# Graph layers beside an attention of 128 blocks: layer steps spread over the slots, projection in the pieces' bank, two node buffers, two lent rows in every block with raw tiles

## What is computed

```python
# layers 0, 2, 3: degree-normalized aggregation, then a 128x128 projection
adj_norm = d[:, :, None] * adj * d[:, None, :]        # d = row sum (of adj + eye, |adj + eye|, or adj) ** -0.5
f = einsum('bnm,bmf->bnf', adj_norm, x) @ W + b
# layer 1: additive attention, masked where adj <= 0
q, k = x @ WQ, x @ WK
score[i, j] = p . relu(q[j] + k[i])                   # 2048 x 2048 x 128 terms for each graph
f = softmax(score + mask) @ x
```

## Time and profile before

| | |
|---|---|
| median of 3 runs | 13884.19 us (13881.76 to 13884.51) |
| the profiled execution's span | 13883.0 us |
| TensorE busy | 12956.7 us, 93% |
| VectorE busy | 13327.1 us, 96% |
| ScalarE busy | 12942.7 us, 93% |
| GpSimd busy | 1095.3 us, 8% |
| TensorE's granted clock, mean | 0.989 |

### The profile page before, as it was taken

One profiled execution on the slowest core, in us unless ns is written; L12 is line 12 of the kernel. 1 busy time (PEld: TensorE's weight loads), 2 busy tenths in 40 slices (PEclk: granted clock), 3 DMA queues, 4 the chain that ended last, 5 costly groups with the idle time before them and its releaser, 6 DMA issues.

```text
span 13883.0 us, 318102 instructions
## 1 busy us (share of the span) xinstructions
PE 12956.7 (93%) x143877; PEld 5442.7 (39%) x143877; DVE 13327.1 (96%) x14041; ACT 12942.7 (93%) x8528; POOL 1095.3 (8%) x706
## 2 busy tenths in 40 slices
PE   7889989999899999999999998999989999899988
PEld 3333434443344333444334443344434444333333
DVE  7999999999999999999999999999999999999995
ACT  6999999999999999999999999999999999999994
POOL 0000000010000100010000100001100010000000
PEclk9999999999999999999999999999999999999999
DMA  4111112221122112221122211222112221011103
GB/s 144 52 46 49 50 58 84 89 63 44 61 90 90 59 37 74 86 87 56 44 72 86 84 59 37 77 87 84 59 36 82 84 80 58 32 49 52 43 12 111
DMA packets 680284, 918.70 MB, mean 66 GB/s; under 512 B 60432, under 2 KB 421904, under 8 KB 659472
## 3 DMA queue, kind: packets, MB, share of 16 engines
q1 hardware_dynamic: 678928, 898.35, 20.7%
HBM read 705.23 MB, written 184.55 MB: 64 GB/s over the span
## 4 chain that ended last, share of the span: by engine, by line
DVE 56%; PE 34%; ACT 7%; issue 2%; DMA 1%; POOL 0%; SPq 0%; DVEq 0%; POOLq 0%; ACTq 0%
DVE big L1110 50%; PE score L1269 24%; ACT big L861 6%; PE acc L1183 5%; PE acc L1242 2%; PE turn L1154 2%; DVE att L1048 2%; DVE big L1090 1%; DVE gx L997 1%; DMA piece<-adj_turned 0%; DVE gx L976 0%; PE turn L1213 0%; DVE stats L984 0%; ACT q_pair L769 0%; DVE att L1037 0%
## 5 line engine op out<-in xcount | busy, mean ns | idle before, releaser
L1110 DVE TENSOR_SCALAR big<-q_pair,k_pair_cols 128x2048 f32<-128x2048 f32 x10029 | 12094.2, 1278 | 289.8 <-PE score L1269 272.4
L861 ACT ACTIVATE big<-q_f,k_cols 128x2048 f32<-128x2048 f32 x6060 | 11633.5, 1998 | 256.9 <-PE score L1269 247.5
L1269 PE MATMUL score<-big,unit_window 128*32 128x512 f16 x82592 | 5439.0, 394 | 750.3 <-DVE big L1110 716.7
L1269 PE MATMUL score<-big,sign_window 128*32 128x512 f32 x48480 | 5591.5, 595 | 69.2 <-ACT big L861 67.5
L1269 PEld LDWEIGHTS score<-big,unit_window 128*32 128x32 bf16 x82592 | 2308.1, 96 | 3952.0 <-DVE big L1110 1128.8
L1269 PEld LDWEIGHTS score<-big,sign_window 128*32 128x32 f32 x48480 | 1572.3, 110 | 3299.2 <-issue 2948.4
L1183 PE MATMUL acc<-piece,q_f 128*128 128x512 f32 x2944 | 1411.5, 602 | 18.1 <-DVE q_f L959 10.7
L668 POOL TENSOR_SCALAR att_var<-att_mom 128x1 f32<-128x1 f32 x128 | 73.4, 573 | 9809.0 <-DVE att_mom L1066 9809.0
L1183 PEld LDWEIGHTS acc<-piece,q_f 128*128 128x128 f32 x2944 | 503.1, 190 | 529.8 <-issue 470.2
L1242 PE MATMUL acc<-x,att_turned 128*128 128x128 f32 x4096 | 559.4, 280 | 0.0
L1242 PEld LDWEIGHTS acc<-x,att_turned 128*128 128x128 f32 x4096 | 504.1, 194 | 56.8 <-issue 56.8
(11 more groups left out here) (95 smaller groups left out, 2876.3 us busy)
## 6 DMA issues: line engine op xcount, KB each, us to landing
piece<-adj_turned SPq DMA_DIRECT2D x1472, 256.0 KB, 2.7
att<-in_adj_dram SPq DMA_DIRECT2D x128, 1024.0 KB, 5.2
q_pair<-in_adj_dram SPq DMA_DIRECT2D x240, 512.0 KB, 4.5
adj_turned<-q_pair SPq DMA_DIRECT2D x224, 512.0 KB, 4.8
adj_turned<-big SPq DMA_DIRECT2D x16, 1024.0 KB, 13.5
q_f<-in_adj_dram SPq DMA_DIRECT2D x16, 512.0 KB, 5.4
gx<-in_x_dram SPq DMA_DIRECT2D x32, 256.0 KB, 4.0
q_kept<-q_pair SPq DMA_DIRECT2D x32, 256.0 KB, 3.7
```

Source lines behind the costliest of these rows:

```text
L861: ins = nc.scalar.activation(ring["A"][:, RANK[g] % RING * 4 + u, :], q_of(c + 1), ACT.Relu, bias=k_cols[:, t % 2, QUAD * u + g:QUAD * u + ...
L1110: ins = nc.vector.tensor_scalar(ring["D"][:, RANK[g] % RING * 4 + u, :], pairs_of(c + 1), k_pair_cols[:, t % 2, QUAD * u + g:QUAD * u + g ...
L1269: ins = nc.tensor.matmul(score[QUAD * u:QUAD * (u + 1), cc, :], (unit_window if pair else sign_window)[:, QUAD - 1 - g:2 * QUAD - 1 - g], ...
```

## The change

The steps get places of their own. `STEP_END` gives for each step the place of its projection (70, 106, ... 454, each a slot); its 16 pieces are spread evenly over the slots from four places after the end before it (the first from 38) up to its own end, two or three to a slot. So twelve steps take 416 places instead of 384, and each slot in between has pieces, while the end slot itself has the projection. Copy and projection are at the end, the sum three or four places later, root, normalization and store at 5, 12, 13 after the end, and the second part of layer 0 (queries, keys) is moved to slots likewise. GpSimd's row beside the sum is in the group ahead of it instead of group 30. ScalarE's sum of a raw unit that would fall less than five places after an end is put to five after it. The projection goes to acc[1] in the batches with attention, so that a step's first piece waits for the sum of the step before, and `weigh` and `project` lose their waits on each other. `gx` and `x1` become two buffers that swap by batch; `keep_x1` goes; `load_x2` is one load for each step, three at place 28 and the last at 34. Every block with raw tiles lends two rows, 126 in all.

```diff
@@ -62,14 +62,55 @@
...
-    BLOCK = {"layer2": 2, "layer3": 6, "layer0": 10}
-    PIECES_AT = {-4: [0, 1, 2], 0: [3, 4, 5], 1: [6], 4: [7], 10: [8, 9], 14: [10], 18: [11], 23: [12, 13, 14, 15]}
-    SELF_AT, TURNED_AT, PROJECT_AT, SUM_AT, ROOT_AT, NORM_OUT_AT, STORE_AT = 18, 28, 28, 31, 33, 40, 41
-    SCALE_AT = {"layer2": [-25, -20, -15, -10], "layer3": [-5, -3, -1, 11], "layer0": [-5, -3, -1, 16]}
-    BIAS_AT, FIRST_LOAD_AT = 20, -8
...
-    X1_AT, X2_AT, X0_AT = 28, 34, 45
+    LAYERS = ("layer2", "layer3", "layer0")
+    STEP_END = {"layer2": [70, 106, 142, 174], "layer3": [210, 247, 279, 316], "layer0": [352, 384, 422, 454]}
+    FIRST_PIECE_AT = 38
+    ALL_SLOTS = [t * GROUPS + at for t in range(T) for at in SLOTS]
+    ENDS = [STEP_END[name][s] for name in LAYERS for s in range(STEPS)]
+    assert all(end in ALL_SLOTS for end in ENDS)
+
+    def slots_of(k):
+        first = FIRST_PIECE_AT if k == 0 else ENDS[k - 1] + 4
+        return [at for at in ALL_SLOTS if first <= at < ENDS[k]]
+
+    PIECE_PLACE = {(name, s): [slots_of(n * STEPS + s)[i * len(slots_of(n * STEPS + s)) // T] for i in range(T)]
+                   for n, name in enumerate(LAYERS) for s in range(STEPS)}
+
+    PROJECT_TIME = 5
+
+    def slot_from(place):
+        return min(at for at in ALL_SLOTS if at >= place)
+
+    def sum_offset(end):
+        return 4 if end % GROUPS == 0 else 3
+
+    SUM_PLACE = {(name, s): STEP_END[name][s] + sum_offset(STEP_END[name][s]) for name in LAYERS for s in range(STEPS)}
+    ROOT_AFTER, NORM_OUT_AFTER, STORE_AFTER, X0_AFTER, BIAS_BEFORE, LOAD_BEFORE = 5, 12, 13, 17, 8, 4
+    SCALE_PLACE = {"layer2": [31, 33, 35, 37],
+                   "layer3": [STEP_END["layer2"][-1] + at for at in (-1, 1, 3, 15)],
+                   "layer0": [STEP_END["layer3"][-1] + at for at in (-1, 1, 3, 20)]}
+    LOAD_PLACE = {"layer2": FIRST_PIECE_AT - 8, "layer3": STEP_END["layer2"][-1] - LOAD_BEFORE,
+                  "layer0": STEP_END["layer3"][-1] - LOAD_BEFORE}
+
+    def qk_places(s):
+        at = {"turn": slot_from(STEP_END["layer0"][s] + 17)}
+        at["copy"] = at["turn"] + 3
+        at["q"] = slot_from(at["turn"] + 4)
...
+        at["k"] = slot_from(at["q"] + 4)
...
+        return at
+
+    QK = [qk_places(s) for s in range(STEPS)]
+    X2_AT, X2_LAST_AT = 28, 34
...
 
...
@@ -292,7 +337,7 @@
         def lent_rows(c, t):
             if not units_where(c, lambda u: slot_place(2 * u) // GROUPS == t):
                 return []
-            return LENT_ROWS[:1 if steps_at(c, t * GROUPS + SELF_AT, SELF_AT) else 2]
+            return LENT_ROWS
 
         def lent_before(c, t, g):
             return sum(len(lent_rows(a, k)) for a in range(FIRST, c + 1) for k in range(T) if a < c or k < t) + \
@@ -350,7 +395,8 @@
 
         def sum_place(u):
             k = 2 * u
-            return k // len(SLOTS) * GROUPS + SUM_UNIT[SLOTS[k % len(SLOTS)]]
+            at = k // len(SLOTS) * GROUPS + SUM_UNIT[SLOTS[k % len(SLOTS)]]
+            return max([end + PROJECT_TIME for end in ENDS if end < at < end + PROJECT_TIME], default=at)
 
         def units_where(c, holds):
             if one_of(c, OPENING, LAST, CLOSING):
@@ -471,7 +523,7 @@
                 n = piece_of(c, name, s, i)
                 if n >= STEPS * T + PIECES:
                     sp.wait_ge(piece_used, piece_of(c, name, s, i, 1 - PIECES + AHEAD))
-                b = {"layer2": c, "layer3": c, "layer0": c + 2}[name]
+                b = batch_of(c, name)
                 sp.dma_start(piece[:, i % PIECES, :], adj_turned[b * (STEPS * T) + (s * T + i)]) \
                     .then_inc(piece_loaded[i % PIECES], 16)
 
@@ -494,28 +546,15 @@
             def load_x0(c, s):
                 if not one_of(c, OPENING, FIRST):
                     sp.wait_ge(out_stored, (c * STEPS + s + 1) * 16 + AHEAD)
-                if not one_of(c, OPENING):
-                    sp.wait_ge(x1_ready, (c + 2) * 16)
-                sp.dma_start(gx[:, s * PER:(s + 1) * PER, :], nodes[c + 2, :, s * PER:(s + 1) * PER, :]) \
+                sp.dma_start(nodes_of(c)[:, s * PER:(s + 1) * PER, :], nodes[c + 2, :, s * PER:(s + 1) * PER, :]) \
                     .then_inc(gx_loaded[s], 16)
 
-            def load_x2(c):
+            def load_x2(c, s):
+                sp.wait_ge(acc_free, block_of(c, 0) + AHEAD)
                 for i in range(2):
-                    sp.wait_ge(x2_stored[i], (c + 1) * (T // 2 * 16) + AHEAD)
-                if one_of(c, CLOSING):
-                    sp.wait_ge(out_stored, c * (STEPS * 16) + AHEAD)
-                else:
-                    sp.wait_ge(x1_ready, (c + 2) * 16)
-                for s in range(STEPS):
-                    sp.dma_start(gx[:, s * PER:(s + 1) * PER, :], x2_nodes[c, :, s * PER:(s + 1) * PER, :]) \
-                        .then_inc(gx_loaded[s], 16)
-
-            def keep_x1(c):
-                sp.wait_ge(layer_output, step_of(OPENING, "layer0", STEPS) if one_of(c, FIRST) else
-                           c * (3 * STEPS) + 2 * STEPS)
-                if not one_of(c, FIRST):
-                    sp.wait_ge(acc_free, block_of(c, 0) + AHEAD)
-                sp.dma_start(x1[:], gx[:]).then_inc(x1_ready, 16)
+                    sp.wait_ge(x2_stored[i], c * (T // 2 * 16) + ((s + 1) * PER // 2 * 16 + AHEAD))
+                sp.dma_start(nodes_of(c)[:, s * PER:(s + 1) * PER, :], x2_nodes[c, :, s * PER:(s + 1) * PER, :]) \
+                    .then_inc(gx_loaded[s], 16)
 
             def store_x2(m, t):
                 sp.wait_ge(att_output, m + 1 + AHEAD)
@@ -549,34 +588,31 @@
                     load_raw(c, u + 1)
...
-                for name, s in steps_at(c, place, FIRST_LOAD_AT):
-                    if s == 0 and not one_of(c, OPENING):
+                for name in side_layers(c):
+                    if place == LOAD_PLACE[name] and not one_of(c, OPENING):
...
                         for i in range(PIECES):
                             load_piece(c, name, 0, i)
-                for at in PIECES_AT:
-                    for name, s in steps_at(c, place, at):
-                        for i in PIECES_AT[at]:
-                            i += PIECES
-                            if s + i // T < STEPS and not one_of(c, OPENING):
-                                load_piece(c, name, s + i // T, i % T)
-                for name, s in steps_at(c, place, STORE_AT):
+                for name, s, i in pieces_at(c, place):
+                    i += PIECES
+                    if s + i // T < STEPS and not one_of(c, OPENING):
+                        load_piece(c, name, s + i // T, i % T)
+                for name, s in steps_at(c, place, STORE_AFTER):
                     if name == "layer3":
                         sp.wait_ge(layer_output, step_of(c, "layer3", s) + 1)
                         sp.dma_start(out[c, s * BANK:(s + 1) * BANK, :].rearrange("(t p) f -> p t f", p=P),
-                                     gx[:, s * PER:(s + 1) * PER, :]).then_inc(out_stored, 16)
+                                     nodes_of(c)[:, s * PER:(s + 1) * PER, :]).then_inc(out_stored, 16)
                 if "layer2" in side_layers(c):
-                    if place == X1_AT and not one_of(c, CLOSING):
-                        keep_x1(c)
-                    if place == X2_AT:
-                        load_x2(c)
+                    for s in range(STEPS):
+                        if place == (X2_LAST_AT if s == STEPS - 1 else X2_AT):
+                            load_x2(c, s)
                 if "layer0" in side_layers(c):
                     if not one_of(c, OPENING):
                         for s in range(STEPS):
-                            if place == start_of("layer3", s) + X0_AT:
+                            if place == STEP_END["layer3"][s] + X0_AFTER:
                                 load_x0(c, s)
                         if place == DIAG_AT:
                             sp.wait_ge(degrees_ready, c + 2)
@@ -786,7 +821,7 @@
                 n = step_of(c, name, s)
                 if n > 0:
                     act.wait_ge(layer_projected, n)
-                summed = units_where(c, lambda u: sum_place(u) < start_of(name, s) + TURNED_AT)
+                summed = units_where(c, lambda u: sum_place(u) <= STEP_END[name][s])
                 if summed:
                     act.wait_ge(raw_abs_summed, unit_of(c + 2, max(summed)) + 1)
                 act.wait_ge(piece_used, piece_of(c, name, s, T, AHEAD))
@@ -1104,9 +1143,8 @@
                                 masked_scores(n)
                             if (g, u) == POOL_ROW and has_pool_row(c, t):
                                 continue
-                            if (g, u) == SUM_ROW and has_sum_row(c, t):
+                            if u == SUM_ROW_PART and g in sum_row_group(c, t):
                                 continue
-
                             ins = nc.vector.tensor_scalar(ring["D"][:, RANK[g] % RING * 4 + u, :], pairs_of(c + 1),
```

(30 more changed lines are left out.)

73 lines of the change are left out of this document (45 added, 28 removed).

## The result

The changed kernel takes 14055.57 us (median; 14045.26 to 14073.44) against 13882.98 beside it: 1.0126 times as long, 95% interval 1.0111 to 1.014. The forecast was 13941 with a range of 13840 to 14000, so the sign was right and the size was not: +173 us where +57 was expected.

What follows compares the result with a forecast made beforehand. A batch was taken to last VectorE's work plus VectorE's stalls, with ScalarE not waited for. 13883 + 50.4 (lent rows) + 11.4 (steps spread) - 4 (buffer swap) = 13941 us; range 13840 to 14000.

Steps and rivals of the forecast that it cites:

- The walk: VectorE and TensorE followed group by group through a batch's blocks: 40.9 us of stalls against 39.0, six times +11.4 us.
- what would show it: Signs in the changed profile: 126 lent rows, VectorE about 1667 us a batch, ScalarE about 1609, score waits 41 us.
- there TensorE was early anyway: Pieces leaving slots 0, 1, 4 and 28 change no stall, as TensorE was early at those slots.
- up to 12 us of gain from filling block 1: Block 1 filled would regain TensorE's granted clock, 2 us a batch, 12 us at most: 13929 instead of 13941.
- 0 plus or minus 2: Batches at both ends, with one or two layers: taken at 0, between -2 and +2 us each.
- the unfulfilled gain at the closing: At the end three loads and the first pieces go ahead of the last x2 store: -4 us (0 to -6).
- The lent rows, +50.4: 42 more rows on VectorE, made ahead of its group 8 where TensorE waits for it: 42 x 1.20 = +50.4 us.
- It falls in that same stretch, where TensorE has 1.7 us in hand: 0: TensorE's extra work for each lent row, taken as 0.25 us, between groups 4 and 9: priced at 0.
- Projection bank, 0: A step's first piece waits for the sum of the step before; wait met, price 0, at worst 66 us.
- swap, -4: Node buffers swap: dropping the 8 copies of x1 gives 0, earlier loads and pieces at the end -4 us.
- Rival 4: More stalls: each block adds another 1 us from late pieces, sum or copy at end slots: 14019 us, chance 0.08.
- Rival 1: The spread removes stalls: VectorE's wait falls from 39 toward 15 us a batch, 13785 us; chance 0.2 for gains over 0.2%.

Runs made afterwards that it cites:

- experiment 3: The changed kernel plus 16 small identity transposes on TensorE ahead of group 4 of every block: 13998.55 us, ratio 1.0083.
- 5 and 6: The kernel before with the pieces at slots 1 and 4 moved to 6: 13915.89 us; the same plus 16 identity transposes ahead of group 4: 13859.81 us.
- experiment 11: The changed kernel with 16 identity transposes ahead of group 4 and the 84 lent rows of before instead of 126: 13978.7 us, ratio 1.007.
- experiment 9: The kernel before with pieces 8 and 9 at slot 6 instead of 10 and two lent rows in every block with raw tiles: 13882.45 us, ratio 1.0.
- experiment 14: The changed kernel with pieces at 1, 4, 9, 12, 20, 25 and 28, none in the slot right before its projection: 13804.24 us, ratio 0.9945.
- experiment 13: The changed kernel's code with places, bank and lent rows of the kernel before, leaving only the node buffer swap: 13879.17 us, ratio 0.9999.
- experiment 1: The kernel before with two lent rows in every block with raw tiles, step places as before: 13963.16 us, ratio 1.0057.

## Why the prediction was wrong

**The walk held where it looked.** With blocks 2 to 8 nearly rid of the clock's part (experiment 3) the waits by block are 4.4, 4.0, 2.6, 2.8, 2.8, 2.6, 3.0, 4.4, 3.2, 3.2 us in blocks 1 to 10; forecast were 4.3, 3.4, 2.1, 2.9, 2.4, 1.9, 2.8, 4.4, 3.05, 3.05. D27's wait is nearly gone and D14, D17 and D22 have theirs, as listed under what would show it. VectorE's busy time (1667 forecast, 1666.47), ScalarE's (1609, 1610.17) and 126 rows came out. The lengths did not: blocks 2 to 8 grew by 2.3 us on average where about 1 was forecast (1.4 in experiment 3), and block 1 by 1.6 where 3 to 4 was.

**The step that failed** is the half sentence on the pieces at 0, 1, 4 and 28: "there TensorE was early anyway". I took work in an idle gap as free to go. It was what held the clock. Taken from 1 and 4, it left 2.2 us bare ahead of D4, D4 ran at 1.2 GHz in 29 of 42 blocks, and two or three pieces (with self in blocks 4 and 5) now stood between it and D9, where the moved idle time had been the reserve. Beside the sum, the only word on the clock had the sign wrong: up to 12 us of gain from filling block 1. The walk itself had no clock at all; it followed TensorE with durations from a block whose granted clock was 1.00. What the step is worth: 57 us filled (experiment 3), and 56 in the kernel before (5 and 6). The Trainium skill ("TensorE: Matmul & The Clock Gate", why this matters for your kernels) says that idle gaps between matmuls drop the clock. The traces agree with that; but the gaps that the page warns of are longer than the 2.2 us here, so it would not have named this one.

**The rest of the 115 us missing.** With experiment 3 the time is 13999, still 58 over the forecast. The six batches hold 37 of it (16.5 us each over before, forecast 10.3): block 11 waits 5.9 us instead of 4.55 and block 12 4.0 instead of 2.2, both by 1.5 to 1.6 us ahead of D9 and D11. The walk began at D9 as if TensorE were always ahead there. In these blocks it is not: three pieces stand at 6, and without raw tiles there is no lent row that brings VectorE later to D9. That is read from the plan; experiment 11, where the lent rows are taken away from blocks 3 to 8 and the same wait comes, bears it out. The last batch holds 11, which I had set to 0 plus or minus 2: it has layer steps in blocks 1 to 9 and the same stalls (VectorE's waits for scores there are 22.8 us before and 32.4 in experiment 3), so it had to be walked too. The first batch holds 5, and the unfulfilled gain at the closing about 5, of which a shorter opening gives 3 back: the three loads still issue behind the store (VectorE's three waits for them are 3.46, 0.64 and 3.33 us).

**The lent rows, +50.4.** As a term by itself nearly right at a full clock (44 us in experiment 9: 1.2 a row in six of seven blocks), and wrong as a term of a sum: the same 42 rows cost 80 us alone in the kernel before, where the clock falls, 20 in the filled change, and nothing that stands clear of noise in the change (-14) and in experiment 14's plan (-10). "It falls in that same stretch, where TensorE has 1.7 us in hand: 0" missed that a later D9 means a longer idle time of TensorE, 2.79 us, and a slow D9.

**Projection bank, 0; swap, -4.** The swap alone costs and brings nothing clear of noise (experiment 13), so the -4 us did not come. The bank has no run of its own; in the batch shown of the changed kernel TensorE idles ahead of none of the 384 piece matmuls and none of the 96 of the projections. GpSimd's rows beside the sums are waited for 9.2 us a batch instead of 2.4, by TensorE, which the walk had in part.

**The rivals.** Rival 4 (more stalls, 14019, chance 0.08) was nearest in its number, and that is luck. Its sign, idle time growing "before A groups or at pieces", did not show: TensorE's waits for ScalarE's rows fell from 5.4 to 1.7 us a batch and grew ahead of D groups. Its mechanisms, late pieces and copies at the end slots, were not the cause. Rival 1 was wrong for these slots and right for others: experiment 14 has 14.9 us of waits in a batch, the 15 that it named, and 13804 us where it had 13785.

## What to carry to other kernels

Before moving work out of a place where an engine waits anyway, ask what the gap does once bare: here 2.2 to 2.8 us of idle time on TensorE ahead of a dense stretch were followed by a group at half the clock, up to 1.5 us longer, in 24 to 29 of 42 blocks, and the price shows two groups later on another engine. A plan of side work is made from the row of gaps and not from an even spread: the same sixteen pieces a step cost 218 us more at 0, 6, 10, 14, 18, 23 and 28 than at 1, 4, 9, 12, 20, 25 and 28. And work shifted between two engines need not cost its own time: the same 42 rows cost from 80 us to nothing, by what waited at their place.

## What was not expected of the hardware

- The clock falls after gaps that look small in a busy share: 2.19 us of idle time ahead of D4 in a block in which TensorE is busy 95%. It doesn't always: of two identical gaps of 2.19 us one was followed by 1.00 and one by 0.53. With 1.7 us (ahead of D9 in the kernel before) no slow stretch is seen in blocks 3 to 8 of the six batches (36 blocks), with 2.79 (experiment 1) in 23 of them. The kernel before also has gaps of 2.1 to 2.8 us ahead of D9, in its blocks 9 to 13, and ten slow stretches in those 30 blocks.
- A slow stretch is short: D4 took 3.54 instead of 2.00 us, and the group behind it, 3.60 us, ran at the full clock again.
- Sixteen transposes of the identity, 1.97 us, were enough to hold it: 24 slow stretches to none (5 and 6).
- GpSimd's small operations on one column slowed without an edit to them: the variance 573 to 992 ns, the root 1527 to 2208 ns (means of 128). They take 572 to 576 ns for the variance in every run with the step places of before, experiment 13 with the changed code included, and 991 ns or more in every run with the spread. So it goes with the places, not with the swap or the lent rows; beyond that the cause is open. The one wait of VectorE for the root, 1.0 us, is the same before and after.
